# Cross-attention in split fp32r: the low part of the keys ahead of the split of the queries, and the split moved behind later maxima

## What is computed

```
x    = layernorm(hidden) * gamma + beta          # 2 x 512 x 1024
Q    = split_heads(x @ Wq.T)
K, V = split_heads(ctx), split_heads(ctx)        # 2 x 1024 x 1024
p    = softmax(where(mask, Q K^T / sqrt(32), -inf))
out  = hidden + (p V, heads merged) @ Wout.T
```

## Time and profile before

| | |
|---|---|
| median of 3 runs | 737.66 us (734.58 to 739.43) |
| the profiled execution's own time | 736.95 us |
| its span, first to last instruction | 735.1 us |
| TensorE busy, mean granted clock | 94% of the span, 0.978 |
| VectorE, GpSimd, ScalarE busy | 66%, 54%, 48% |

### The profile page before, as it was taken

The page is one execution under the profiler, slowest core; times in us unless marked ns, Lnnn a source line. Parts: engine busy times, 40 slices in busy tenths (PEclk is TensorE's granted clock), DMA queues, the critical chain, the costliest instruction groups (busy, mean ns, idle before and its releaser), DMA issues.

```text
span 735.1 us, 10854 instructions
## 1 busy us (share of the span) xinstructions
PE 692.0 (94%) x3585; PEld 397.1 (54%) x3585; DVE 483.0 (66%) x494; ACT 351.1 (48%) x614; POOL 394.1 (54%) x107
## 2 busy tenths in 40 slices
PE   2789999978999999999999999999999999999998
PEld 2578788534444444444444445444444444478886
DVE  6763432157688878878788887888878776653231
ACT  3741211434566666566666666666666656600000
POOL 1000000047296797967979679796797978930000
PEclk9799999979899999999999999999999999999999
DMA  9621100425426144161441614416244202213231
GB/s 339 180 65 36 44 14 1 119 50 128 100 61 158 38 123 110 51 157 37 122 109 50 157 40 120 111 48 157 49 109 94 84 14 88 86 66 122 98 114 57
DMA packets 39519, 68.10 MB, mean 93 GB/s; under 512 B 5285, under 2 KB 21799, under 8 KB 39471
## 3 DMA queue, kind: packets, MB, share of 16 engines
q1 hardware_dynamic: 39444, 67.64, 33.7%
q10 hardware_dynamic: 36, 0.01, 0.0%
HBM read 25.18 MB, written 4.19 MB: 40 GB/s over the span
## 4 chain that ended last, share of the span: by engine, by line
PE 84%; DVE 6%; SPq 4%; ACT 2%; DMA 2%; issue 2%; POOL 0%; ACTq 0%; DVEq 0%; POOLq 0%
PE SX L914 18%; PE MX L894 17%; PE PV L930 16%; PE MX L1058 12%; PE SM L920 6%; PE PV L857 5%; PE SM L857 4%; DVE mx L715 3%; PE MX L834 2%; SPq L303 1%; SPq L311 1%; DMA PR<-in_x 1%; PE SX L849 1%; PE MX L906 1%; PE MX L900 1%
## 5 line engine op out<-in xcount | busy, mean ns | idle before, releaser
L715 DVE TENSOR_REDUCE mx<-MX 128x1 f32<-128x1024 f32 x256 | 303.2, 1221 | 139.0 <-PE MX L894 138.7
L592 ACT ACTIVATE PR<-SX 128x512 f32<-128x512 f32 x512 | 277.4, 594 | 186.2 <-PE SX L914 186.0
L470 POOL TENSOR_TENSOR acc<-acc,PR 128x2048 f32<-128x2048 f32 x64 | 293.5, 4586 | 31.5 <-ACT PR L592 25.1
L470 POOL TENSOR_TENSOR acc<-PR 128x2048 f32<-128x2048 f32 x16 | 73.3, 4579 | 222.5 <-ACT PR L592 143.3
L914 PE MATMUL SX<-R 99*128 99x512 f32 x512 | 180.7, 432 | 3.2 <-ACT PR L592 2.9
L894 PE MATMUL MX<-R 97*128 97x512 f32 x512 | 165.0, 419 | 15.9 <-DVE mx L715 7.1
L914 PEld LDWEIGHTS SX<-R 99*128 99x128 f32 x512 | 88.7, 190 | 113.8 <-ACT PR L592 93.8
L894 PEld LDWEIGHTS MX<-R 97*128 97x128 f32 x512 | 89.6, 190 | 104.1 <-DVE mx L715 65.0
L930 PE MATMUL PV<-PR,C 128*32 128x512 f32 x1024 | 138.9, 615 | 0.1
L803 DVE TENSOR_TENSOR PR<-PR,MX 128x512 f32<-128x512 f32 x16 | 10.9, 687 | 53.3 <-PE MX L1058 51.8
L1058 PE MATMUL MX<-R 128*128 128x512 f32 x192 | 44.3, 390 | 0.0
(11 more groups left out here) (77 smaller groups left out, 520.3 us busy)
## 6 DMA issues: line engine op xcount, KB each, us to landing
R<-KTh SPq DMA_DIRECT2D x64, 256.0 KB, 4.3
PR<-in_x SPq DMA_DIRECT2D x16, 512.0 KB, 4.1
C<-in_ctx SPq DMA_DIRECT2D x16, 512.0 KB, 3.4
R<-KTl SPq DMA_DIRECT2D x64, 128.0 KB, 3.9
R<-QT SPq DMA_DIRECT2D x64, 128.0 KB, 2.5
acc<-in_L_xattn_Wq SPq DMA_DIRECT2D x8, 512.0 KB, 3.5
R<-QT SPq DMA_DIRECT2D x64, 64.0 KB, 2.1
C<-in_L_xattn_Wout SPq DMA_DIRECT2D x8, 512.0 KB, 3.3
```

Of the source, the lines that this page charges most:

```text
L470: nc.gpsimd.tensor_tensor(acc[:, :, :], a, PR[:, tt % RING, :, :], ALU.add).then_inc(pool_used, 1)
L592: nc.scalar.activation(PR[:, tt % RING, h, :], SX[h % 2][:, :], ACT.Exp, scale=SCALE).then_inc(exp_done, 1)
L715: nc.vector.tensor_reduce(mx[:, u % 2, c:c + 1], MX[par][:, :], mybir.AxisListType.X, ALU.max, negate=True).then_inc(mx_freed, 1)
```

## The change

In each step VectorE makes the keys' low part where it split the queries first, and the split, now two functions `query_high` (the cast) and `query_low` (the subtraction), comes later: in the loop and in step 13 the cast behind maximum 4 and the subtraction behind maximum 6; in step 0 behind maxima 7 and 9. SP's queue waits for the keys alone ahead of the keys' DMAs, and for the queries ahead of theirs. The instructions are the same ones in number and shape, and so are their semaphores. Ahead of step 0 nothing moves.

```diff
--- before.py
+++ after.py
@@ -321,9 +321,9 @@
 
             def stack(n, u):
 
-                queries_split(n)
                 keys_split(n)
                 key_rows(u % RING)
+                queries_split(n)
                 query_rows(u % RING)
 
             def bias_rows(n, u):
@@ -699,13 +699,19 @@
             for i in range(KCH, 2 * KCH):
                 split_x(i)
 
-            def split_queries(n):
+            def query_high(n):
                 if not is_first(n):
                     dve.wait_ge(queries_in, STACKED * n)
-                q = QA[:, bass.ds(n, 1), :].rearrange("p a s -> p (a s)")
-                nc.vector.tensor_copy(QTh, q).then_inc(qt_hi, 1)
+                nc.vector.tensor_copy(QTh, QA[:, bass.ds(n, 1), :].rearrange("p a s -> p (a s)")).then_inc(qt_hi, 1)
+
+            def query_low(n):
                 dve.wait_ge(qt_hi, n + 1)
-                nc.vector.tensor_tensor(QTl, q, QTh.bitcast(F32), ALU.subtract).then_inc(qt_lo, 1)
+                nc.vector.tensor_tensor(QTl, QA[:, bass.ds(n, 1), :].rearrange("p a s -> p (a s)"), QTh.bitcast(F32),
+                                        ALU.subtract).then_inc(qt_lo, 1)
+
+            def split_queries(n):
+                query_high(n)
+                query_low(n)
 
             def maximum(n, u, i, par):
 
@@ -766,8 +772,6 @@
                         invert_sums(n - 1, sums_at.index(tt))
                     for kind, a, i in items[tt][0] + items[tt][1]:
                         if kind == "keys":
-                            if a == 2:
-                                split_queries(n + a)
                             key_low(n + a, at % 2)
                         if kind == "bias":
                             bias_low(n + a, at % 2)
@@ -775,6 +779,11 @@
                             wout_parts(i, at % 2)
                         if kind == "max":
                             maximum(n + a, u + a, i, at % 2)
+                            if a == 1 and n + 2 < STEPS:
+                                if i == (7 if first else 4):
+                                    query_high(n + 2)
+                                if i == (9 if first else 6):
+                                    query_low(n + 2)
                         at += 1
 
             step(0, 0, FIRST_STEP, FIRST_PARITY, first=True)
```

## The result

The changed kernel takes 789.13 us (median of 6 runs, 784.47 to 791.29) against 737.83 us before (6 runs): the ratio is 1.0695, with a 95% interval of 1.0669 to 1.072. That is slower, by 51 us, where 28 were forecast.

What follows compares the result with a forecast made beforehand. TensorE, busy 94% of the 735.1 us span, was taken as the bound. 13 steps x 2.2 = 28.6 us plus 0.3 for step 0, 28.9 on 736.95, gave 765.9, stated as 766; range 744 to 774.

Steps and rivals of the forecast that it cites:

- part 4: Subtraction behind maximum 6 waits for GpSimd's first add, takes 3.3 us; maximum 10 is 2.2 us late in 13 steps.
- the lock: Subtraction behind maximum 6 waits for the end of GpSimd's first add, ending 0.55 us after it; chance 0.81.
- the first rival: Subtraction shares with the add, takes 1.65 us; maximum 10 0.6 us late in 13 steps, about 745 us; chance 0.09.
- the stretch now is at 1.00, and I assume that a pause of 2 us leaves it there: TensorE's granted clock in the loop stays at 1.00 despite the 2 us pause; no cost included.
- from there its work is only shifted: TensorE behind the late maximum 10 keeps its old spacing, so the whole step is 2.2 us longer.
- +0.3 us: Step 0, split behind maxima 7 and 9: between 1.7 us gained at best and 2.2 lost at worst.
- The bound of 2.2 us from above: Step 0: at worst the subtraction runs into the add beginning at 167.89 and costs 2.2 us.
- The parts costed at nothing: Keys' low part 0.1 us earlier with nobody waiting, DMA order 0, cast behind maximum 4 with TensorE not waiting.
- GpSimd's second add: In each loop step, it was to begin 0.5 us later behind the first add, as a sign of being right.

Runs made afterwards that it cites:

- e10: Changed kernel, in steps 1 to 13 the slot 3 scores of heads 2 and 3 by one fp32 matmul each instead of fp32r: 776.2 us.
- e7: Changed kernel, GpSimd's first add of steps 1 to 15 over 384 of 512 columns of each head: 755.1 us, ratio 1.0245.
- e1: Changed kernel, in steps 1 to 13 the subtraction right behind the cast, behind maximum 4: 742.1 us, ratio 1.0076.
- e6: Changed kernel, subtraction right behind the cast, behind maximum 4, and step 0 in the order of the kernel before: 738.4 us, ratio 1.0017.
- e2: Kernel before, with SP's queue alone as in the changed kernel, keys' DMAs waiting for the keys only: 738.5 us, ratio 1.0019.
- e8: Kernel before, last of three instructions inverting the sums moved behind maxima 1 to 3 of slot 7, steps 1 to 14: 736.8 us, ratio 0.9997.
- e11: Kernel before, maximum 3 moved from slot 7 to the next step's slot 0, ahead of the keys: 743.8 us, ratio 1.0095.
- e9: Kernel before, four short matmuls of 8 columns more in slot 3 of steps 1 to 15: 757.9 us, ratio 1.0285.

## Why the prediction was wrong

The sign was right, and so was the cause of the wait; the size was not: 766 us were forecast, in a range up to 774, and 789 came.

- **The wait (part 4) was right in its cause and size, and nearly in its place.** It was to be 2.2 us a step from a subtraction of 3.3 us; the trace has 3.49 us, maximum 10 late by 2.1, and e10's sum over 12 steps at full clock gives 2.1. e7 cut the add and shortened the wait by as much. The forecast had TensorE idle ahead of maximum 10 alone; in the trace most of the idle time, 1.24 us, stands ahead of maximum 9, which needs the buffer of the late maximum 7, and 0.40 us ahead of maximum 10. Choosing the lock against the rate of the first rival was right, and the Trainium skill's rule ("SBUF — State Buffer", section "SBUF: two separate sides") agrees with the trace for this subtraction too: it ends 0.54 us behind the add, in the changed kernel and in e7.
- **The step that failed is "the stretch now is at 1.00, and I assume that a pause of 2 us leaves it there", and with it "from there its work is only shifted".** The prediction named the clock as the place where a term might be missing and gave it no price. It costs 1.6 us in ten of the twelve steps between the marks, 16 us: values in 1.84 us instead of 1.00, scores and maximum 10 likewise. Rows of the kernel before could have priced it; they are of step 0, slot 7, with a maximum in each of the first three:

```profile
181.99 0.73 PE L894 MATMUL MX<-R 97*128 97x512 f32 x2 [0.41 <-DVE mx L715]
183.31 0.73 PE L894 MATMUL MX<-R 97*128 97x512 f32 x2 [0.58 <-DVEq L723]
184.62 1.22 PE L894 MATMUL MX<-R 97*128 97x512 f32 x2 [0.58 <-DVE mx L715]
...
187.10 1.94 PE L930 MATMUL PV<-PR,C 128*32 128x512 f32 x8
```

Behind idle gaps of 0.41, 0.58 and 0.58 us the group of values lasts 1.94 us at the lower clock, and 1.06 elsewhere. With that term for ten to thirteen steps the forecast would have been 782 to 787.
- **Step 0 was mis-sized.** +0.3 us was taken for it, "nearer the loss"; it measured 3.9 to the mark of step 1, and e1 less e6 gives 3.7. By TensorE's busy time some 1.9 of it (26.4 less 24.5) are work at the lower clock, so the term left out above is missing here as well. The step looked at the subtraction, and it was the cast that met an add: the earlier keys brought it to 167.62, and the add had begun at 167.55. The bound of 2.2 us from above was too low, since a cast that comes up at an add's start waits for all 4.6 us of it.
- **The parts costed at nothing cost nothing**: the order of the DMAs (e2), the keys' earlier low part and the cast behind maximum 4 (e6).
- GpSimd's second add was to begin 0.5 us later. In the trace it begins on time (375.36) and takes 4.79 us instead of 4.59: the same wait for the subtraction's end, but 0.2 us, and shown as duration.

By terms, in the profiled execution: in the 12 steps waits 25 and clock 16, up to the mark of step 1 4 (about half of it clock), step 13 and the end 2, together 47.6 us.

Open is what decides whether the clock falls. Steps 1, 9 and 13 of the changed kernel have the same pause (in step 13 1.16 and 0.40 us) and kept the upper level. Windows of step 1 and, for comparison, of step 10:

```profile
196.74:229.21 32.47, 30.47 (x165) 14.04 (x165) 25.66 (x23) 19.26 (x35) 24.35 (x6) 1.00 0.35 86
...
501.85:535.93 34.08, 32.06 (x165) 14.65 (x165) 25.69 (x23) 19.26 (x35) 24.39 (x6) 0.95 0.35 86
```

and the two waits in step 1, maximum 9 and maximum 10:

```profile
207.95 0.73 PE L903 MATMUL MX<-R 97*128 97x512 f32 x2 [1.23 <-DVE mx L721]
209.08 0.73 PE L903 MATMUL MX<-R 97*128 97x512 f32 x2 [0.40 <-DVE mx L721]
```

They are 1.23 and 0.40 us, those of the step shown above to 0.01 us, and this step takes 32.47 us at a clock of 1.00. So the pause makes the fall possible and doesn't fix it. Nor is it shown why the other five runs, with a median of 789.4 us, take 5.0 us more than the profiled one: their mean granted clocks, 0.950 to 0.961, lie on both sides of its 0.956.

## What to carry to other kernels

Before a VectorE instruction on two SBUF tensors (or an SBUF to SBUF cast) is moved, look at what GpSimd does at the new place: its price there is the rest of GpSimd's instruction. Here the same two instructions cost nothing beside an idle GpSimd (e6) and the kernel takes 47 us more with one of them two maxima later (e1 against the changed kernel). When a wait of one or two microseconds falls on a TensorE that was hardly ever idle, price the work behind it at the lower clock too, as one end of the range. And idle time that remains on a full engine may be the tail of another chain: e8 and e11 moved what stood beside it and not its cause.

## What the runs showed of the hardware

- **Length of TensorE's loop.** Sixteen matmuls more in the body of the loop (four in each of four steps, e9) made each of its two turns 7 to 8 us longer and took the instruction queue from 17 to 35 packets, 0.28 to 0.57 MB; e10 had nine packets more and one long turn. That is 16 KB a packet and nine packets for a long turn. The Trainium skill ("Runtime: NRT & Kernel Launch", section "Instruction fetch mechanics") describes an instruction memory for each engine that is refilled in blocks of 16 KiB, and says that a jump to code outside it has to wait for the fetch; the packets and the 3.55 us of "issue" agree with both. What length still fits was not measured: the body of the kernel before is within it, and that of e10, whose two turns differ, seems to be at its edge.
- **A short pause and the clock.** Idle gaps of 1.24 and 0.40 us next to each other were followed by some 3 us at 1.2 GHz in ten of thirteen steps. With 0.40 us ahead of maximum 10 and no more than 0.1 ahead of maximum 9 they were in none: in e7 the steps from 1 to 12 have a clock of 1.00 and take 31.2 to 31.4 us (32.1 and 32.2 at the loop's turns), and in e10 they have it but for its long turn.
- **Constant rest behind GpSimd.** Subtractions that waited 1.0, 1.7 and 2.8 us ended 0.55, 0.54 and 0.54 us behind GpSimd's end.
